# Attention and feed-forward layer: x loaded once and kept on chip for the residual sum

## The reference

```python
def block(x, Wq, bq, Wk, bk, Wv, bv, Wo, bo, weight):
    n = layernorm(x)
    q, k, v = (heads(n @ W.T + b) for W, b in ((Wq, bq), (Wk, bk), (Wv, bv)))
    scores = where((j <= i) & (j >= i - 128), q @ k.T * 0.25, -10000.0)
    attn = softmax(scores) + 1e-9
    x = x + (attn @ v) @ Wo.T + bo
    return x + layernorm(x) @ sign(weight).T
```

## Time and profile before

| | us |
|---|---|
| median of three runs | 712.52 |
| the runs | 704.73, 712.52, 713.14 |
| the profiled execution | 706.15 |
| its span | 704.3 |

### The profile page before, as it was taken

The page is one execution under the profiler, slowest core; times in us unless marked ns, Lnnn a source line. Parts: engine busy times, 40 slices in busy tenths (PEclk is TensorE's granted clock), DMA queues, the critical chain, the costliest instruction groups (busy, mean ns, idle before and its releaser), DMA issues.

```text
span 704.3 us, 31680 instructions
## 1 busy us (share of the span) xinstructions
PE 664.0 (94%) x13152; PEld 593.9 (84%) x13152; DVE 493.5 (70%) x1043; ACT 485.4 (69%) x1061; POOL 458.8 (65%) x651
## 2 busy tenths in 40 slices
PE   7789999999999999999999999999999999999796
PEld 6667988888988889889898889888898888888685
DVE  5566766787777777777677777777777776777545
ACT  4357776777767678777767767676776776677472
POOL 8936565786656577565667756566765655776484
PEclk9989999999999999999999999999999999999998
DMA  5947776786677885787687866767776966677331
GB/s 154 129 78 134 107 122 114 138 132 119 120 126 124 114 138 112 130 126 122 119 128 139 131 99 126 127 133 122 121 129 120 133 120 110 137 129 115 67 60 54
DMA packets 94942, 83.76 MB, mean 119 GB/s; under 512 B 10416, under 2 KB 94800, under 8 KB 94800
## 3 DMA queue, kind: packets, MB, share of 16 engines
q1 hardware_dynamic: 93354, 80.38, 67.2%
q10 hardware_dynamic: 1446, 1.35, 0.6%
HBM read 18.22 MB, written 8.39 MB: 38 GB/s over the span
## 4 chain that ended last, share of the span: by engine, by line
PE 73%; DMA 12%; SPq 6%; issue 3%; DVE 3%; ACT 2%; POOL 1%; DVEq 0%; POOLq 0%; ACTq 0%
PE gc L1061 17%; PE sc L1197 16%; PE pv L1216 11%; PE ga L1061 10%; DMA q_stack<-nmax_t 10%; SPq L273 6%; PE mx L1152 5%; PE mx L1158 4%; PE ga L1229 3%; PE gc L1076 2%; DVE nmax L831 2%; PE gb L1245 2%; PE gb L1265 2%; DMA q_stack<-q_hi 1%; ACT prob L604 1%
## 5 line engine op out<-in xcount | busy, mean ns | idle before, releaser
L604 ACT ACTIVATE prob<-sc 128x512 f32<-128x512 f32 x448 | 259.6, 599 | 98.7 <-PE sc L1197 94.9
L831 DVE TENSOR_REDUCE nmax<-mx 128x6 f32<-128x960 f32 x189 | 197.1, 1043 | 68.2 <-PE mx L1158 66.1
L1197 PE MATMUL sc<-q_stack,k_stack 128*128 128x256 f32 (+1 forms) x1024 | 211.0, 304 | 9.5 <-DMA q_stack<-nmax_t 6.2
L1197 PEld LDWEIGHTS sc<-q_stack,k_stack 128*128 128x128 f32 x1024 | 149.8, 190 | 24.9 <-DMA q_stack<-nmax_t 11.1
L461 POOL TENSOR_SCALAR ve<-mv 128x1 f32<-128x1 f32 x64 | 14.3, 224 | 196.3 <-DVE mv L903 195.3
L440 POOL TENSOR_SCALAR_AFFINE_SELECT prob<-prob 128x1024 f32<-128x1024 f32 x128 | 140.3, 1096 | 1.4 <-ACT prob L604 1.4
L432 POOL TENSOR_SCALAR_AFFINE_SELECT prob<-prob 128x1024 f32<-128x1024 f32 x112 | 122.8, 1096 | 12.4 <-ACT prob L604 12.1
L1216 PE MATMUL pv<-prob,v_ones 128*32 128x128 f32 x3776 | 117.1, 274 | 1.9 <-issue 1.9
L1216 PEld LDWEIGHTS pv<-prob,v_ones 128*32 128x32 f32 x3776 | 99.7, 110 | 10.7 <-issue 2.2
L1158 PE MATMUL mx<-k_max,q_stack 16*32 16x160 bf16 x4032 | 71.1, 229 | 3.9 <-issue 3.9
L1152 PE MATMUL mx<-edges,ident 32*32 32x192 bf16 (+1 forms) x1328 | 44.6, 244 | 9.1 <-issue 5.3
(11 more groups left out here) (172 smaller groups left out, 1429.6 us busy)
## 6 DMA issues: line engine op xcount, KB each, us to landing
q_stack<-q_hi SPq DMA_DIRECT2D x128, 128.0 KB, 3.7
k_stack<-k_hi SPq DMA_DIRECT2D x128, 128.0 KB
xs<-x SPq DMA_DIRECT2D x32, 256.0 KB, 4.4
q_stack<-q_lo SPq DMA_DIRECT2D x64, 128.0 KB
k_stack<-k_lo SPq DMA_DIRECT2D x64, 128.0 KB
xr<-x SPq DMA_DIRECT2D x64, 128.0 KB, 2.0
out<-x SPq DMA_DIRECT2D x64, 128.0 KB, 2.2
k_max<-k SPq DMA_DIRECT2D x64, 64.0 KB, 3.5
```

What stands on the lines that cost most here:

```text
L604: a.activation(prob[:, own:nxt + 1:nxt - own, 2 * f:2 * f + 2, :], sc, ACT.Exp, scale=SCALE).then_inc(exp_done, 1)
L831: v.tensor_reduce(nmax[:, n % 2, :].rearrange("p (r h) -> p r h", r=C)[:, :, h0:h0 + m], banks[:, :, 0:WIN * m].rearrange("p r (h k) -> p ...
L1197: last = mm(sc_bank[f % 2][:, 2 * P * j:2 * P * j + q], k_stack[:, h, ak:ak + P], q_stack[:, h % HB, P * t:P * t + q], start=True, stop=True)
```

## The change

`xs` grows from two pairs to six (`KEPT`), 12 KB per partition instead of 4. `xr`, its two semaphores and all 64 `load_xr` are gone, and with them the wait for x2 that each held on SyncE. Pair g lies at place g mod 6 from its load to its second tile's residual. GpSimd adds the bias row in place, behind `xn_done` of the pair, and the residual reads the sum from there. The load of pair g has a second wait: x2 of both tiles of pair g-6 must be done. The value stack `v_ones` is not touched. PE, ScalarE, VectorE and GpSimd issue the same instructions in the same order.

```diff
@@ -39,6 +39,7 @@
 SUMS = 3 * DK + 1
 SC_FILLS = 8
 AHEAD = 4
+KEPT = 6
 ENDING = 5
 
 MX_GROUPS = ((0, 1, 2), (3, 4, 5), (6, 7))
@@ -80,7 +80,7 @@
         window0 = sb("window0", [P, P // QB, WIN], BF16)
         half = sb("half", [P, 2])
 
-        xs = sb("xs", [P, 2, 2, D])
+        xs = sb("xs", [P, KEPT, 2, D])
         st1 = sb("st1", [P, 2, 6])
         mv1 = sb("mv1", [P, 2, 2])
         ve1 = sb("ve1", [P, 2])
@@ -254,8 +252,11 @@
             def load_x(b, p):
                 i, n = halves(p)
 
-                wait(sp, xn_done, PAIRS * b + p - 1)
-                sp.dma_start(xs[:, i], x_pair[b, p]).then_inc(x_loaded[i], 16)
+                g = PAIRS * b + p
+
+                wait(sp, xn_done, g - 1)
+                wait(sp, x2_done, 2 * (g - KEPT + 1))
+                sp.dma_start(xs[:, g % KEPT], x_pair[b, p]).then_inc(x_loaded[i], 16)
 
             def stack_q(b, p, r):
                 i, _ = halves(p)
@@ -299,12 +300,6 @@
                         sp.dma_start(k_stack[at:at + DK, HB * c:HB * (c + 1), cols].bitcast(F32),
                                      src[:, g % 2, c, :].bitcast(F32)).then_inc(k_stacked[i], 16)
 
-            def load_xr(b, t):
-                i, _ = halves(t)
-
-                wait(sp, x2_done, TILES * b + t - 1)
-                sp.dma_start(xr[:, i], x_tile[b, t]).then_inc(xr_loaded[i], 16)
-
             def store_y(b, t):
                 i, _ = halves(t)
 
@@ -313,8 +308,6 @@
 
             def slot(b, t):
                 now, part = parts(b, t)
-                if part["xr"]:
-                    load_xr(*part["xr"])
                 if part["k"]:
                     for r in range(3):
                         stack_q(*part["k"], r)
@@ -348,15 +341,10 @@
             load_x(0, 3)
             run(sp, slot)
             stack_k(LAST, 3)
-            load_xr(LAST, 3)
             stack_nmax(sp, LAST, 7)
-            load_xr(LAST, 4)
             store_y(LAST, 1)
-            load_xr(LAST, 5)
             store_y(LAST, 2)
-            load_xr(LAST, 6)
             store_y(LAST, 3)
-            load_xr(LAST, 7)
             store_y(LAST, 4)
             store_y(LAST, 5)
             store_y(LAST, 6)
@@ -448,10 +436,11 @@
 
             def add_biases(b, t):
 
-                i, n = halves(t)
+                g_pair, j = (TILES * b + t) // 2, t % 2
                 pool.wait_ge(brow_done, b + 1)
-                pool.wait_ge(xr_loaded[i], 16 * (TILES // 2 * b + n + 1))
-                g.tensor_tensor(xr[:, i], xr[:, i], brow[:, :], ALU.add).then_inc(xb_done, 1)
+                pool.wait_ge(xn_done, g_pair + 1)
+                kept = xs[:, g_pair % KEPT, j]
+                g.tensor_tensor(kept, kept, brow[:, :], ALU.add).then_inc(xb_done, 1)
 
             def rsqrt2(b, t):
                 n = TILES * b + t
@@ -535,7 +524,7 @@
 
                 wait(act, t1_filled, n)
                 for j in range(2):
-                    last = a.activation(xn[:, j], xs[:, i, j], ACT.Identity, bias=nmr1[:, j:j + 1], scale=rs1[:, j:j + 1])
+                    last = a.activation(xn[:, j], xs[:, n % KEPT, j], ACT.Identity, bias=nmr1[:, j:j + 1], scale=rs1[:, j:j + 1])
                 last.then_inc(xn_done, 1)
 
             def xt_part(b, p, bank=gc):
@@ -790,7 +779,7 @@
 
                 wait(dve, mv1_done, n)
                 for j in range(2):
-                    last = v.bn_stats(st1[:, j], xs[:, i, j])
+                    last = v.bn_stats(st1[:, j], xs[:, n % KEPT, j])
                 last.then_inc(bn1_done, 1)
                 dve.wait_ge(bn1_done, n + 1)
                 wait(dve, xn_done, n)
@@ -888,7 +877,7 @@
 
                 wait(dve, y_stored[i], 16 * (TILES // 2 * b + m))
                 dve.wait_ge(xb_done, n + 1)
-                v.tensor_tensor(x2[:, i], ga[:, 0:D], xr[:, i], ALU.add).then_inc(x2_done, 1)
+                v.tensor_tensor(x2[:, i], ga[:, 0:D], xs[:, n // 2 % KEPT, t % 2], ALU.add).then_inc(x2_done, 1)
 
             def stats2(b, t):
                 i, _ = halves(t)
```

More of the change, by code:

```diff
@@ L52, in build @@
     x_pair = x.rearrange("b (g t p) d -> b g p t d", t=2, p=P)
-    x_tile = x.rearrange("b (t p) d -> b t p d", p=P)
     y_tile = out.rearrange("b (t p) d -> b t p d", p=P)
@@ L120, in build @@
         cb = brow[:, :].rearrange("p (c q) -> p c q", c=C)
-        xr = sb("xr", [P, 2, D])
         x2 = sb("x2", [P, 2, D])
@@ L152, in build @@
         nmax_stacked = [sem("nmax_stacked0"), sem("nmax_stacked1")]
-        xr_loaded = [sem("xr_loaded0"), sem("xr_loaded1")]
         y_stored = [sem("y_stored0"), sem("y_stored1")]
@@ L225, in parts @@
                 now = (b, t)
-            return now, {"nm": tile(2), "mx": tile(3), "pv": tile(-1), "xr": tile(-2), "op": tile(-3), "ff": tile(-4),
+            return now, {"nm": tile(2), "mx": tile(3), "pv": tile(-1), "op": tile(-3), "ff": tile(-4),
                          "tqv": pair(5), "k": pair(4), "ks": pair(1), "ln": pair(6), "load": pair(7)}
```

## The result

| | before | after |
|---|---|---|
| median, us | 712.64 | 714.82 |
| of 20 runs each, from and to | 703.83 to 716.06 | 708.84 to 719.75 |
| ratio, 95% interval | 1 | 1.0098 (1.0071 to 1.0126) |
| the same kernel measured again (`a_again`) | 1 | 1.0046 (1.0008 to 1.0084) |

What follows compares the result with a forecast made beforehand. TensorE (PE) was taken as the bound. 706.15 less 9.7 us of row-maxima stalls, all else nothing, gave 696.5, or 702.8 if the run spread remains; the forecast was 699, range 691 to 709.

Steps and rivals of the forecast that it cites:

- The waits for the row maxima go: Score products on PE: all 18 stalls, 11.1 us on weight loads, vanish because the q burst starts 1.8 us earlier.
- the 9.7 of the sum: Gain in us forecast from removing PE's stalls on the row maxima, the only term not counted at nothing.
- In an odd slot: SyncE's k transfers, row maxima and load of x move about 2.1 us earlier; counted as worth nothing.
- really starts earlier: Even slot's q burst on SyncE starts at 305.56 instead of 307.36, since the DMA engines are idle in between.
- The loads of xr cost only their DMA time: Removing 64 loads of 128 KB frees 0.44 us of SyncE each and a tenth of queue q1's traffic.
- the 0.65 I named: Forecast DMA share if the prediction was right, a tenth lower than before.
- The load of x gets a wait that costs nothing: SyncE, odd slots: new wait on x2 of two tiles has 4 us of room, so no cost.
- Rival 3: Slower: the new wait at the load of x stops SyncE's queue, 712 to 728 us; chance 0.05.
- GpSimd, the tail: GpSimd's in-place bias addition and the run's end, set by the last tile's residual: both counted at nothing.
- Rival 1: More goes than this trace's waits: late landings behind the run spread vanish too, 690 to 698 us; chance 0.25.
- Rival 2: Time given back as PE waits for ScalarE or VectorE; gain 0 to 3 us, 703 to 712; chance 0.22.
- 0.70 for 0.80: A score product's loss of 0.70 us per 0.80 charged to its weight load, used to scale 11.1 to 9.7.

Runs made afterwards that it cites:

- e2_deep_xr: Kernel before with xr four tiles deep instead of two, so the slot-head wait is met at once and all loads stay: ratio 0.9961, 694.3 us at full clock.
- e3_head_even: Changed kernel with the old wait for x2 put back at the head of even slots only: ratio 1.0011, 698.8 us at full clock.
- e4_head_odd: Changed kernel with the old wait for x2 put back at the head of odd slots only: ratio 1.0014, 700.2 us at full clock.
- e9_shift: Changed kernel with 60 more warming transposes at the start of PE's program: ratio 1.0122 in two runs.
- e1_head: Changed kernel with the old wait for x2 back at every slot's head, nothing loaded behind it: ratio 1.0009, 695.7 us at full clock.
- e11_dummy: Changed kernel with an unread 128 KB load at each slot's head, no wait for x2: ratio 0.9968, 694.8 us at full clock.
- e13_small: Changed kernel with an unread 16 KB load at each slot's head, no wait for x2: ratio 1.0026, 696.6 us at full clock.
- e7_less_k: Changed kernel without the third part of the k stack, two of six k transfers left out: ratio 0.9985, 699.2 us at full clock.
- e8_paced: Changed kernel with row maxima first in every slot and stacking transfers split by waits on score products: ratio 0.9980, 700.1 us at full clock.
- e12_head_nmmid: Changed kernel with the slot-head wait back and row maxima issued between the q_hi and q_lo transfers: ratio 0.9901, 691.1 us at full clock.

## Why the prediction was wrong, step by step

*The waits for the row maxima go.* Right: from 11.1 us to none, and 0.10 us from the y store to the first q transfer where I said 0.04. The lead was real, and `e2_deep_xr` shows that it is worth 3 us where nothing else changes, less than the 9.7 of the sum: it has 4.1 us more page stalls and 6.6 more of "issue" in all than before, so part was given back there already.

*"In an odd slot ... I count it at nothing; its cover is that these landings are already in time", and of the even slot that the burst "really starts earlier".* This is the step that failed. I looked at whoever waits on a semaphore of the moved transfers, found none, and took the idle stretch of the DMA engines (0.08 busy) for waste. One more user of those engines has no semaphore in the program: PE's own instructions. The term that was missing, page stalls, measures 24.6 - 9.6 = 15.0 us between the two profiles, or 21.5 - 9.6 = 11.9 with `a_again`. With it the sum is -11.1 + 11.9 and, for the reduction's waits below, + 4.6: 5.4 us slower, where the time at full clock says about 5 for that measurement. So near a match is in part luck: smaller waits fell by 2.2 us, so all stalls of the weight loads together rose by 3.2 us in `a_again` (65.0 to 68.2) and by 7.9 in after (72.9). That the even and the odd slots share it is shown by `e3_head_even` and `e4_head_odd`; that the stalls are pages, by `e9_shift`; that more of them come when nothing holds the burst off at the slot's head, by `e1_head`, and by `e2_deep_xr`, `e11_dummy` and `e13_small`, where a load stands there. That it is the packing of the bursts, and not the moment at which they start, is argued: every kernel with shorter bursts (`e7_less_k`, `e8_paced`) moved their start too.

The rows were there. The "issue" stalls made up 28.7 us in the trace of before, more than twice the row maxima (9.6 of them page stalls, and 17.5 at the bound products of L1152), the instruction queue is on the page, and I passed over both.

*The loads of xr cost only their DMA time.* Wrong in sign. The DMA share fell to 0.69 and not to the 0.65 I named, and their absence is part of the loss: put back with nobody to read them they are worth 8 us. In the profile of that kernel page stalls are 5.2 us fewer than in `a_again` and the reduction's waits 5.6, so only a part of it is pages.

*The load of x gets a wait that costs nothing.* Right. SyncE never waits for the residual there; the only wait at that line is the old one on the norm, once:

```profile
SPq L259 <- ACT xn L527: 5.1, 1, 5.1
```

Rival 3 with its 0.05 did not happen; the sign came out its way by another mechanism, for which I had no rival.

*GpSimd, the tail.* Nothing, as said.

*Rival 1, that the spread of the runs is late landings which the lead removes.* It fell. The runs' times follow their granted clock (correlation -0.73 to -0.97 in the kernels with ten runs or more), and the spread after is as wide as before. The changed kernel has no more half clock than the one before, but one stretch of it began right behind a page stall. Around the stall that ended at 206.33, by microsecond (the figure behind those of the five engines is the granted clock):

```profile
205.00:206.00 1.00, 0.00 (x0) 0.00 (x0) 1.00 (x2) 0.27 (x1) 0.46 (x1) 1.00 1.17 122
206.00:207.00 1.00, 0.67 (x25) 0.67 (x28) 1.00 (x3) 0.00 (x0) 0.00 (x0) 0.98 0.52 131
207.00:208.00 1.00, 1.00 (x28) 1.00 (x23) 0.00 (x0) 0.00 (x0) 0.00 (x0) 0.50 0.06 19
```

PE had stood still for 1.64 us, and the clock is at half, 1.2 of 2.4 GHz, from 207 to 210. Not every page stall is followed by this: `a_again` has 24 of them and 11.4 us at half clock in all.

*Rival 2, time given back at the next wait.* Partly right, with the wrong weight. The waits for the exponential did not grow (4.0 to 3.7 us), those for VectorE's maxima did, over all rows from 8.5 to 11.4 and 13.1 us. They grew more in `e12_head_nmmid`, to 15.8, which is the fastest kernel. Why they grow is not settled by these runs, and they are 4.6 us of the sum above.

*What stays open.* The page stalls explain most of the loss, not all differences: `e11_dummy` has 16.3 us of them and is faster at full clock than `e1_head` with 12.5, each from one profile. And the trace doesn't show why the packet is late. Counted from PE's last passing of a block's end, half of the packets start within 1.3 us, before and after alike; the late ones are later, with the 90th percentile at 2.8 us before, 3.6 after and 3.3 in `a_again`. The packets themselves hardly take longer (median 1.63 and 1.67 us). Whether a late one stands behind the data in the engine that carries it, or its request is served late, is not shown.

## What to carry to other kernels

Before a transfer is moved into a stretch where the DMA engines look idle, read who uses them without a semaphore: the instruction queue on the page, and the "issue" stalls in the list of waits. If such stalls sit at constant steps of the instruction count they are pages of the program, and here an earlier start of the bursts made more of them. An issue of 0.4 us ahead of a burst, or a small urgent transfer put in the middle of one, was worth more here than the earlier start. And two edits that each gain may lose together, so a change that takes out a wait and the load behind it should be costed, and run, as three kernels.

## What the runs showed of the hardware

PE's program came through the same DMA engines as the data, in packets of 16 KB that took 1.63 us in the median before and 1.67 after, one for 125 weight loads and matmuls. Where PE ran dry it went on 1.2 to 2.0 us after the packet's end: at 206.33 after 204.74 and at 429.10 after 427.84 in after, at 502.12 after 500.57 in before. The 17 profiles have 5 to 25 us in about 700 of such stalls; PE's program is the same but for `e9_shift`, and mostly the order and the timing of the transfers differ.

Over all profiles but `e9_shift`, with its 60 further transposes, the time of the execution less all stalls of the weight loads and less half of the time at half clock is 630 to 635.5 us, while the stalls range from 58 to 76. So a us of stall on the weight loads was about a us of time, which is more than I had allowed with 0.70 for 0.80. This holds for all stalls together; page stalls by themselves follow the time less closely (correlation 0.65, against 0.95).
